# Causal masks of 64 rows: each head parity's masks by its own half of the array

## The reference

```python
att = jnp.einsum('bhqd,bhkd->bhqk', q, k) * scale
causal = jnp.tril(jnp.ones((T, T), bool))
att = jnp.where(causal[None, None], att, -jnp.inf)
y = jnp.einsum('bhqk,bhkd->bhqd', jax.nn.softmax(att, axis=-1), v)
...
attc = jnp.einsum('bhqd,bhkd->bhqk', qc, kc) * scale
y = y + jnp.einsum('bhqk,bhkd->bhqd', jax.nn.softmax(attc, axis=-1), vc)
```

## Time and profile before

| | |
|---|---|
| median of three runs | 378.12 us |
| the three runs | 374.95, 378.12, 379.81 us |
| profiled execution, its own time | 374.34 us |
| its span, first to last instruction | 372.6 us |
| time outside the span | 1.7 us |
| mean granted TensorE clock | 0.948 |
| busy: PE, DVE, ACT, POOL | 326.8, 233.9, 191.7, 110.0 us |

### The profile page before, as it was taken

The page is one execution under the profiler, slowest core; times in us unless marked ns, Lnnn a source line. Parts: engine busy times, 40 slices in busy tenths (PEclk is TensorE's granted clock), DMA queues, the critical chain, the costliest instruction groups (busy, mean ns, idle before and its releaser), DMA issues.

```text
span 372.6 us, 7109 instructions
## 1 busy us (share of the span) xinstructions
PE 326.8 (88%) x2696; PEld 188.9 (51%) x2696; DVE 233.9 (63%) x546; ACT 191.7 (51%) x397; POOL 110.0 (30%) x202
## 2 busy tenths in 40 slices
PE   4689799979999999789989799999987599899994
PEld 2446433424434344244476467677755266565662
DVE  5889998858888879466442143332213679649765
ACT  3267388858898888557248323322247143323220
POOL 5526231316433233123575003443350201100000
PEclk9999879989999999899989699999998599989999
DMA  7759792960323005230161560000004000000001
GB/s 177 172 124 210 132 195 56 213 187 4 115 74 102 4 2 173 73 102 3 26 214 35 128 184 10 18 23 21 10 21 118 0 0 3 0 0 2 28 1 28
DMA packets 35777, 27.80 MB, mean 75 GB/s; under 512 B 5579, under 2 KB 33022, under 8 KB 35744
## 3 DMA queue, kind: packets, MB, share of 16 engines
q1 hardware_dynamic: 33574, 25.27, 27.4%
q0 software_dynamic: 1280, 1.88, 1.6%
q10 hardware_dynamic: 890, 0.20, 0.3%
HBM read 11.89 MB, written 5.26 MB: 46 GB/s over the span
## 4 chain that ended last, share of the span: by engine, by line
PE 69%; DVE 13%; ACT 6%; DMA 4%; issue 4%; POOL 2%; ACTq 1%; SPq 0%; POOLq 0%; DVEq 0%
PE psum L1468 12%; PE psum L1672 11%; PE psum L1703 7%; PE psum L1691 4%; DVE nmax L1042 4%; PE psum L1434 4%; PE psum L1650 4%; PE psum L1410 3%; PE psum L1486 3%; PE psum L1402 3%; ACT ot_sb L818 2%; PE psum L1412 1%; PE psum L1655 1%; PE psum L1765 1%; PE psum L1437 1%
## 5 line engine op out<-in xcount | busy, mean ns | idle before, releaser
L1042 DVE TENSOR_REDUCE nmax<-psum 128x2 f32<-128x1024 f32 (+2 forms) x88 | 103.2, 1216 | 15.6 <-PE psum L1410 11.3
L843 ACT ACTIVATE parts<-psum 128x512 f32<-128x512 f32 (+1 forms) x88 | 44.7, 569 | 9.3 <-PE psum L1434 8.8
L1672 PE MATMUL psum<-p_more,kcat 128*128 128x320 f32 x128 | 42.6, 475 | 0.7 <-DVE p_more L1176 0.7
L1185 DVE TENSOR_TENSOR qcat<-psum,qk_r 128x320 f32<-128x320 f32 x32 | 15.7, 491 | 42.8 <-ACT qk_r L886 42.6
L733 POOL DMA_INDIRECT rows_back<-qcat,back_at x24 | 22.9, 953 | 53.1 <-ACT qcat L876 48.2
L886 ACT ACTIVATE qk_r<-psum 128x320 f32<-128x320 f32 x32 | 14.0, 437 | 45.2 <-PE psum L1672 45.2
L1703 PE MATMUL psum<-h_t,kcat 128*128 128x512 f32 x64 | 30.9, 608 | 0.7 <-ACT h_t L854 0.7
L1410 PE MATMUL psum<-kcat,qcat 64*128 64x512 bf16 x128 | 25.9, 404 | 5.5 <-DVE nmax L1042 4.8
L1672 PEld LDWEIGHTS psum<-p_more,kcat 128*128 128x128 f32 x128 | 23.4, 200 | 13.5 <-issue 4.6
L1468 PE MATMUL psum<-parts,v_aug 128*9 128x256 f32 (+1 forms) x352 | 28.9, 373 | 0.0
L1434 PE MATMUL psum<-qcat,kcat 64*128 64x256 bf16 x256 | 25.6, 280 | 3.0 <-ACT p_more L843 1.2
(11 more groups left out here) (225 smaller groups left out, 609.5 us busy)
## 6 DMA issues: line engine op xcount, KB each, us to landing
kcat<-parts SPq DMA_DIRECT2D x18, 192.0 KB, 4.1
qcat<-parts SPq DMA_DIRECT2D x24, 128.0 KB, 3.9
kcat<-ones_b SPq DMA_DIRECT2D x8, 192.0 KB, 5.2
kcat<-in_L_ffn_wi_gate_dram SPq DMA_DIRECT2D x6, 256.0 KB, 3.8
kcat<-in_L_ffn_wi_up_dram SPq DMA_DIRECT2D x6, 256.0 KB, 4.0
kcat<-in_L_ffn_wo_dram SPq DMA_DIRECT2D x6, 256.0 KB, 5.5
parts<-in_L_ffn_w_dram SPq DMA_DIRECT2D x3, 512.0 KB, 5.5
rows_in<-zeros SPq DMA_DIRECT2D x1, 1290.0 KB, 5.8
```

What stands on the lines that cost most here:

```text
L843: act.activation(p_slots[u % NPT][:, 0:w], s2_bank(s2_place[u])[:, 0:w], ACT.Exp, scale=SCALE).then_inc(p_in, 1)
L1042: dve.tensor_reduce(dst[:, :, n * g:n * (g + 1)], src.rearrange("p (r q k) -> p r q k", r=PAR, q=n), AX.X, ALU.max, negate=True).then_inc( ...
L1185: dve.tensor_tensor(hh[:, e % 2, f, 0:SLOTS], bank(3 + 2 * (i % 2))[:, 0:SLOTS], sg[:, i % 2, 0:SLOTS], ALU.mult).then_inc(hh_in[0], 1)
L1672: ins = pe.matmul(bank(2 + 2 * (i % 2) + m)[:, 0:SLOTS], w_t[e][:, m, f * P:(f + 1) * P], xs_t[:, e % 2, :], start=True, stop=True)
```

## The change

The identity and the mask get twice the width. `ident_w` has 64 columns of zeros on either side of the identity, `mask_w` is the causal pattern over 256 columns, shifted by 64. `ident_b`, which the turn units use, is now the middle of `ident_w`. Each mask of a head is no longer one product of 128 rows but two of 64 rows that use only the half of the array (and of the constants' partitions) that the head's scores use. In the first turn the half adds one half of the mask's rows, in the second, with both constants read 64 columns further left, the other. The products of the two parities alternate. The number of mask products goes from 4 to 8 in a late unit and from 8 to 16 in an early one.

`bv_wide`, a bias copy that is read only at the start, gives up its own memory and uses the beginning of `got`, which is loaded late in the kernel.

```diff
-        bv_wide = sb("bv_wide", [P, D])
...
-        ident_b = sb("ident_b", [P, P], BF16)
-        mask_b = sb("mask_b", [P, P], BF16)
+        ident_w = sb("ident_w", [P, 2 * P], BF16)
+        mask_w = sb("mask_w", [P, 2 * P], BF16)
+        ident_b = ident_w[:, P // 2:P // 2 + P]
...
         got = sb("got", [P, 2, NT, D])
+        bv_wide = got[:, 0, 0, :]
...
+            link(pool.memset(ident_w[:, :], 0.0))
             const(pool.tensor_copy(ident_b[:, :], ident[:, :]))
-            link(pool.memset(mask_b[:, :], 0.0))
-            const(pool.affine_select(out=mask_b[:, :], in_=mask_b[:, :], pattern=[[-1, P]], compare_op=ALU.is_ge,
-                                     fill=NEG, base=0, channel_multiplier=1))
+            link(pool.memset(mask_w[:, :], 0.0))
+            const(pool.affine_select(out=mask_w[:, :], in_=mask_w[:, :], pattern=[[-1, 2 * P]],
+                                     compare_op=ALU.is_ge, fill=NEG, base=P // 2, channel_multiplier=1))
...
                 if kind != "cross":
-                    for par in range(PAR):
-                        dst, w = bank(first + par), BANK // heads
+                    w = BANK // heads
+                    for turn in range(2):
                         for n in range(heads):
-                            pe.matmul(dst[:, (n + 1) * w - P:(n + 1) * w], ident_b[:, :], mask_b[:, :],
-                                      start=(n == 0), stop=False, skip_group_check=True)
+                            for par in range(PAR):
+                                rows = slice(64 * par, 64 * par + 64)
+                                shift = slice(64 * (1 + par - turn), 64 * (1 + par - turn) + P)
+                                pe.matmul(bank(first + par)[:, (n + 1) * w - P:(n + 1) * w], ident_w[rows, shift],
+                                          mask_w[rows, shift], start=(turn == 0 and n == 0), stop=False,
+                                          skip_group_check=True)
```

## The result

| | before | changed |
|---|---|---|
| median of 15 runs each | 377.91 us | 374.93 us |
| lowest to highest | 374.91 to 379.84 | 371.42 to 381.60 |
| mean of all 15 | 377.79 | 375.65 |
| profiled execution (span), mean clock | 374.34 (372.6), 0.948 | 378.54 (376.8), 0.938 |

The stated ratio is 0.9899 (95% interval 0.9870 to 0.9929), 1.0% faster. It leaves out slow runs, which are 5 of the 15 of the changed kernel and none of the 15 of before, so it flatters the change. Over all 15 runs of each the means differ by 2.15 us, with a standard error of 0.86 (each group's spread over the root of 15, the two squared, added and rooted). On a second chip, with 12 and 23 runs (e8), the ratio is 0.9943 (0.9911 to 0.9974). Both speak for a small gain, near 2 us.

A forecast was written before the change was run, and what follows sets the result against it. TensorE was taken to bound the kernel, with 69% of the chain that ended last. Gains of 0.29 us (part 0) and 1.42 us (parts 3 to 7), 1.7 us off a base of 376.5, gave 374.8 us; range 371.6 to 378.8.

The forecast's parts named there:

- What bounds the stretch: From part 5 to part 6, TensorE is the tightest engine, busy 15.12 of 15.80 us; the others have 2.4 us to spare.
- The price of the new products: Masked units: 0.030 us per half-height product, 0.24 us to the first score in a late unit, 0.46 to 0.48 early.
- Part 0, 0.29 us: Three masked units of part 0: VectorE waits for the early scores, so their gain passes through, 0.29 us.
- Part 1, 0: Part 1: VectorE is busy without a break for 12.81 us, so TensorE's gain becomes a longer wait, 0.
- Part 2, 0: Part 2: the gain goes into the 2.36 us wait at 78.05 for the maxima's transfer, queued behind SyncE's others, 0.
- Parts 3 to 7, 1.42 us: Parts 3 to 7: 15 masked units, all in the chain, gain 0.095 us each, 1.42 us in all.
- The constants, 0: GpSimd's memsets at the start: at most 0.9 us more, covered by 7.75 us of idle time, cost 0.
- VectorE at the early reduction: Part 5: VectorE's idle time before the early reduction falls from 0.42 to about 0.2 us, so the gain passes.
- The base and the range: Whole kernel: base 376.5 us, the middle of four known times; range 371.6 to 378.8 us from the spread.
- A: Masked units: products start only each 0.057 us, a part is 0.62 us longer, 380.2 us in all; chance 0.08.
- B: Between masks and scores: the 0.10 us gap belongs to a shared bank, not height, and stays; 376.5 us, chance 0.15.
- C: Behind the wait at 78 us: one more or denser half-clock stretch eats 1.4 us of the gain; 376.2 us, chance 0.12.

The follow-up runs named there:

- e8: The changed kernel again, no further edit, beside runs of the kernel before on the same chip: mean 372.16 us, ratio 0.9943 to the kernel before.
- e5: The changed kernel with one more full-height product, adding zeros, between masks and scores of each masked unit: 374.79 us, timed once.
- e6: The changed kernel with the mask products of one half in a row, then the other's, in place of alternating: 375.48 us, timed once.
- e7: The changed kernel with SyncE's last-batch layout queued behind part 2's maxima and second-turn masks on their last 64 columns only: mean 368.12 us.

## Why the prediction was right, and where it was not

- **What bounds the stretch**, and the gap of 0.10 us from full to half height: right. e5 puts two changes of height in and pays 0.10 us for each.
- **The price of the new products**, taken from L1415: right. 0.23 us and 0.46, where 0.24 and 0.46 to 0.48 were said. The term per unit was 0.095 us and measured 0.106, since the scores behind the masks also end 0.01 us earlier.
- **Part 0, 0.29 us: wrong.** The step that failed is "the three units give 0.29 us". It looked only behind the masks. Ahead of them are full-height products, so the number of changes of height stays the same, and the gap moved from behind the masks to ahead of them.
- **Part 1, 0: right within what can be read.** VectorE's stretch of 11 reductions is 12.64 us long instead of 12.81. Three traces with masks by halves there have 12.63 to 12.68, three with full height 12.76 to 12.90, so it had small holes after all. What it gave ended in the wait at 78 us.
- **Part 2, 0: right.** The wait is the queue's, and with the queue moved part 2's gain comes through. That the wait grows by 0.3 us while its end moves 0.3 us earlier is not borne out: it was 3.34 us in one profile of the changed kernel and 2.15 in the other, and the queue's own length scatters by more than 1 us.
- **Parts 3 to 7, 1.42 us**: 5 x 0.32 = 1.6 us. The missing 0.29 of part 0 and the extra 0.18 here nearly cancel, hence 1.6 for a forecast of 1.7.
- **The constants, 0**: right, 0.8 us more under an idle time of 6.66 us.
- **VectorE at the early reduction**: idle 0.32 us, and 0.2 was said. The second late reduction starts 0.47 us behind the start of its scores, before 0.43: late by 0.04 us, where 0.1 was allowed.
- **The base and the range.** The middle of four known times, less 1.7, gave 374.8; the median is 374.93. That they meet within 0.1 us is luck: the median of 15 runs of the kernel before is 377.9, 1.4 us above the base, and the two medians differ by 3.0 us, 1.3 more than the sum. The forecast of 1.7 us and the 2.15 and 1.9 us of the means agree within their errors; the stated ratio alone would make it 3.8 us. The scatter that the range was built on is real, and with the slope on the granted clock over half of its variance goes (1.5 us to 1.0).
- **Rivals.** A: its 0.057 us is the step of the full-height masks, and the new ones have half of it. At full clock the pairs of masks start 0.056 us apart, and the second pair 0.066 behind the first, so an early unit's 16 masks take 0.46 / 16 = 0.029 us each. B: refuted by the changed kernel's own timeline and by part 0. C: the half-clock stretch behind the wait was 3.4 us longer in one profiled execution of the changed kernel and as long as before (3.4 us) in the other, e8. The traces give the clock as 1.00 and 0.50, the "2.4 GHz" and "1.2 GHz" of the forecast; no trace shows a frequency, and none enters its sums. Over 27 runs the mean clock is 0.950, as over 68 runs of the kernel before.

## What to carry to other kernels

Count the changes of the array's form along TensorE's order, on both sides of the place that is to be changed: a gap saved behind it can come back ahead of it, as the 0.10 us of each unit of part 0 did. Ask of every part of a periodic stretch whether what follows it waits for TensorE or for a queue that has its own pace; here that decided over 9 of 24 units, and the queue was worth more (2.8 us) than the masks (1.9). Do not read the gain off the length of such a wait; it moves with the queue (3.34 and 2.15 us in two profiles of the changed kernel). Where runs scatter with the clock by more than the effect, compare with all runs, on one chip and at equal clock, and read the effect from a period of the trace.

## What the runs showed of the hardware

- A change between full height (128*128) and half height (64*128) costs 0.10 us at a granted clock of 1.00, in both directions (e5: 0.33 - 0.23 and 0.16 - 0.06). It costs 0.09 to 0.11 us where the two sides share no bank (ahead of the masks of part 0: 0.64, 1.10 and 0.64 us from the first projection to the first mask, before 0.54, 0.99 and 0.55).
- Two halves of the array run their own products side by side: 24 loads and products in a row start 0.029 us apart on the mean (117.67 to 118.36 in the changed kernel), where the full-height masks start 0.057 us apart. They need not alternate: four products of one half in a row cost nothing, eight cost 0.25 us, and then a half's later products start ahead of earlier ones of the other half (e6).
- A pair of 64-column products on the two halves costs about half a pair of 128 columns: eight products of the second turn take 0.46 - 0.35 = 0.11 us less than with 128 columns (e7). From pair to pair it is 0.029 us with 64 columns and 0.056 with 128.
- Single issues in SyncE's queue take 1.0 to 1.7 us where the same kind takes 0.6, at other places in each trace (67.18 in the changed kernel, 72.66 before). The queue that ends the wait at 78 us is 17.4 to 18.7 us long from the maxima of part 1 to those of part 2, over the eight traces that have its order.
